# Three weight loads behind waits on VectorE, added on TensorE after each convolution chunk

## What is computed

```python
def attn(u):                                   # (8, 2048, 1024)
    x = u @ W_in + b_in                        # 1024 -> 3072
    uc = dw_causal_conv(x, short_w, short_b)   # 3 taps per channel
    q, k, v = split(uc)
    v = dw_causal_conv(k * v, inner_w, inner_b)  # 4 taps per channel
    return (q * v) @ W_out + b_out
def ffn(x):
    probs = softmax(x @ gate_w.T + gate_b)
    h = relu(x @ w1[e] + b1[e])                # for all e, 1024 -> 2048
    out = h @ w2[e] + b2[e]                    # for all e, 2048 -> 1024
    return sum over the top 2 of probs of out[e] * probs[e]
x = x + attn(layernorm(x))
x = x + ffn(layernorm(x))
```

## Time and profile before

| what | us |
|---|---|
| median of three runs | 2606.03 |
| the three runs | 2765.21, 2595.39, 2606.03 |
| the profiled execution's own time | 2595.71 |
| its span, slowest core | 2594.2 |
| spans of the eight cores | 2588.5 to 2594.2 |
| granted TensorE clock, mean of each core | 0.913 to 0.916 |
| TensorE busy with matmuls | 2214.1 (85%) |
| VectorE busy | 786.5 (30%) |
| ScalarE busy | 444.9 (17%) |

### The profile page before, as it was taken

One profiled execution on the slowest core, in us unless ns is written; L12 is line 12 of the kernel. 1 busy time (PEld: TensorE's weight loads), 2 busy tenths in 40 slices (PEclk: granted clock), 3 DMA queues, 4 the chain that ended last, 5 costly groups with the idle time before them and its releaser, 6 DMA issues.

```text
span 2594.2 us, 24806 instructions; the slowest of 8 cores (2588.5 to 2594.2 us)
## 1 busy us (share of the span) xinstructions
PE 2214.1 (85%) x9840; PEld 1020.3 (39%) x9840; DVE 786.5 (30%) x1346; ACT 444.9 (17%) x784; POOL 24.3 (1%) x81
## 2 busy tenths in 40 slices
PE   1657685622799999999999997699999999999999
PEld 1323231322344444444444444434444444444444
DVE  2086979566211111111111321211211112111121
ACT  1222121111221120211102021130201112021120
POOL 0000000000000000000000000000000000000000
PEclk9968787755799999999999996689999999999999
DMA  8300000300333334554334451033454333554331
GB/s 195 68 1 1 1 1 0 65 1 0 65 65 65 65 65 73 90 89 74 65 66 77 86 93 54 17 66 65 83 94 84 65 66 65 89 90 81 65 65 65
DMA packets 10624, 161.25 MB, mean 62 GB/s; under 512 B 1024, under 2 KB 1152, under 8 KB 6288
## 3 DMA queue, kind: packets, MB, share of 16 engines
q0 software_dynamic: 5968, 142.63, 31.0%
q1 hardware_dynamic: 4544, 17.05, 1.9%
HBM read 293.91 MB, written 8.39 MB: 117 GB/s over the span
## 4 chain that ended last, share of the span: by engine, by line
PE 79%; DVE 8%; issue 7%; DMA 3%; ACT 2%; DVEq 0%; POOL 0%; ACTq 0%; POOLq 0%
PE psum L712 17%; PE psum L757 17%; PE psum L717 17%; PE psum L759 17%; PE psum L500 4%; DMA winbt<-winl 3%; PE psum L369 2%; PE psum L615 1%; DVE tmpBt L564 1%; PE psum L618 1%; ACT ln2tft L358 1%; DVE tmpAt L544 1%; ACT ln2T L356 1%; DVE tmpBt L558 1%; DVE ln2ft L328 1%
## 5 line engine op out<-in xcount | busy, mean ns | idle before, releaser
L757 PE MATMUL psum<-w2bt,hbt 128*128 128x512 bf16 x2048 | 782.8, 382 | 0.8 <-DVE resid L766 0.8
L759 PE MATMUL psum<-w2bt,hbt 128*128 128x512 bf16 x2048 | 782.3, 382 | 0.0
L725 ACT ACTIVATE hbt<-psum,constsf_s 128x1024 bf16<-128x1024 f32 x256 | 285.3, 1114 | 1369.6 <-PE psum L717 1369.6
L712 PE MATMUL psum<-ln2T,w1bt 128*128 128x512 bf16 x2048 | 486.8, 381 | 0.7 <-ACT wbct L455 0.7
L717 PE MATMUL psum<-ln2T,w1bt 128*128 128x512 bf16 x2048 | 483.8, 379 | 0.0
L731 DVE TENSOR_TENSOR hbt<-hbt,wbct 128x1024 bf16<-128x1024 bf16 x256 | 177.3, 692 | 748.4 <-ACT hbt L725 748.4
L766 DVE TENSOR_TENSOR resid<-resid,psum 128x1024 f32<-128x1024 f32 x128 | 156.3, 1221 | 732.6 <-PE psum L759 732.6
L500 PE MATMUL psum<-ln1tt,winbt 128*128 128x512 bf16 x768 | 216.1, 449 | 145.4 <-DVE qkvt L534 104.8
L757 PEld LDWEIGHTS psum<-w2bt,hbt 128*128 128x128 bf16 x2048 | 202.7, 99 | 251.3 <-issue 15.3
L712 PEld LDWEIGHTS psum<-ln2T,w1bt 128*128 128x128 bf16 x2048 | 200.9, 98 | 245.5 <-issue 5.8
L759 PEld LDWEIGHTS psum<-w2bt,hbt 128*128 128x128 bf16 x2048 | 201.6, 98 | 242.8 <-issue 6.5
(11 more groups left out here) (68 smaller groups left out, 663.2 us busy)
## 6 DMA issues: line engine op xcount, KB each, us to landing
w1bt<-w1l POOLq DMA_DIRECT2D x16, 4096.0 KB, 27.5
w2bt<-w2l POOLq DMA_DIRECT2D x16, 4096.0 KB, 27.3
out<-resid SPq DMA_DIRECT2D x16, 512.0 KB, 2.6
winbt<-winl POOLq DMA_DIRECT2D x8, 768.0 KB, 8.4
resid<-u SPq DMA_DIRECT2D x1, 6144.0 KB, 44.3
resid<-u SPq DMA_DIRECT2D x1, 2048.0 KB, 16.9
woutbt<-woutl POOLq DMA_DIRECT2D x1, 2048.0 KB, 14.7
constsf_s<-constsf SPq DMA_DIRECT2D x1, 244.0 KB
```

What stands on the lines that cost most here:

```text
L712: T.matmul(bank(bb), lhs, ln2T[Dc][:, 0:512], start=(Dc == 0), stop=(Dc == DC - 1))
L725: em = s_s.inc(S.activation(hbuf[Hcc][:, :], bank(bb, 1024), AF.Relu, bias=constsf[:, B10 + 16 * e + Hcc:B10 + 16 * e + Hcc + 1]))
L757: T.matmul(bank(bb), lhs, w2B[Hcc][:, 0:512], start=st, stop=(Hcc == HC - 1))
L759: ins = T.matmul(bank(bb + 1), lhs, w2B[Hcc][:, 512:1024], start=st, stop=(Hcc == HC - 1))
```

## The change

A helper `warmers` is added, and `emit_conv` calls it after each chunk's y product. `ym` is the value of VectorE's counter once y is done. For the values `ym - 10`, `ym - 5` and `ym` TensorE gets a wait and then a weight load of the first 128 columns of `selB` (8 partitions, loaded at the start of the program). No matmul uses these weights: each matmul that follows brings its own load. The waits are made directly and not by `Waiter`.

```diff
+        def warmers(sem, upto, n=3, stride=5):
+            for i in range(n - 1, -1, -1):
+                v = upto - i * stride
+                if v > 0:
+                    T.wait_ge(sem.h, v)
+                    T.ldweights(selB[0:8, 0:128])
...
                 y_mark[c] = ym
                 tmp_free = ym
+                warmers(s_v, ym, 3, 5)
                 if chunk_cb is not None:
                     chunk_cb(c)
```

## The result

The changed kernel takes 2687.96 us (median of 10 runs) against 2594.83 us for the kernel before on the same chip. The ratio is 1.0354, 95% interval [1.0341, 1.0368]. The change makes the kernel 3.5% slower, 92 us by this ratio. The forecast was 2690, with a range from 2672 to 2714. Medians are over all runs, while a ratio leaves out the executions in which cores of a die ran longer at a lower granted clock, so that a ratio and the quotient of two medians can differ a little.

What follows compares the result with a forecast made beforehand. The projection's end on TensorE was taken to bound tiles 0 to 2; held behind the last y, they lose 91.9 us, giving 2687.6 from the profiled run or 2697.9 from the median; forecast 2690, range 2672 to 2714.

Steps and rivals of the forecast that it cites:

- What bounds a tile: Attention part, tiles 0 to 2: the input projection's end on TensorE sets the tile's end; delaying it delays everything.
- The waits hold the queue: Tiles 0 to 2: no next-tile projection matmul starts before the last y; 0.25 us from y's end to the first matmul.
- The rival in which a waiting load lets the matmuls pass: TensorE sets waiting weight loads aside, projection runs as before: 2596 to 2606 us, no change; chance 0.03.
- the sign that the forecast named: First projection matmul of tile 1: at 143.6 us if waits do not hold the matmuls, at 225 if they do.
- The length of a burst: After the convolution in tiles 0 to 2: 192 projection matmuls in one burst take 43.6 us.
- the slow start: First matmuls of each projection burst run slower than 0.215 us each, costing between 0 and 2.7 us; 2.0 in the sum.
- the half clock: Projection bursts at half clock throughout: 75 us for 192 matmuls, 32 more a tile, 2783 us; lower burst clock has 0.03.
- 13/16: Peak-current limit of 13/16 of the clock in the bursts: 9.5 us a tile, 2716 us; lower burst clock has 0.03.
- The loads: 96 weight loads at 0.104 us; 23 of a tile's 24 hidden, the last adds 0.1 us; 0 in tile 3.
- The clock held by the loads: Loads keep TensorE's clock at 1.00 over convolution and tile 3's gate pieces: 13 us less, 2674 us; chance 0.04.
- The sum: Delays of 30.0, 31.3 and 30.6 us in tiles 0 to 2, together 91.9, on 2595.71: 2687.6 us.

Runs made afterwards that it cites:

- the new order: Kernel before with the projection's chunks as k, v, q of each chunk in turn, instead of the eight q's last: 2562.14 us against 2596.87, ratio 0.9863.

## Why the prediction was right

- **What bounds a tile.** The step was that the end of the projection on TensorE sets the end of tiles 0 to 2. It held in both directions: ending it later by 30 us cost 92 us in three tiles, ending it about 12 us sooner gained 35 us. With the new order it stopped being so in tile 1, where VectorE's chain ends 0.81 us later.
- **The waits hold the queue.** The forecast had the 192 matmuls of a tile wait for the last y. They did, at 223.86 us on core 0, 0.38 us after y's end at 223.48. The forecast took 0.25 us, with an upper bound of 0.5. The rival in which a waiting load lets the matmuls pass has fallen by the sign that the forecast named: the first projection matmul of tile 1 starts at 223.86 us and not at 143.6. The run with waits only adds that it makes no difference whether a load or a matmul stands behind the wait.
- **The length of a burst.** 43.6 us was forecast, and 43.20, 43.80 and 43.11 were measured. Against 192 x 0.215 = 41.3 us that leaves 1.8 to 2.5 us for the slow start, inside the bound. Both cases of a lower clock in long bursts have fallen, the half clock and 13/16: the granted clock in the burst of tile 0 is 0.96, and 183 of its weight loads took 39.38 us, 0.215 each. One reading was wider than its row: the earlier trace rows is core 7 alone. In the same stretch (83.5 to 125.6 us) cores 1, 2 and 4 have 0.97. The expert part on core 7 has 0.62 from 1600 to 1700 us, around the gate of the second half. Neither changes the sum.
- **The loads.** 0.104 us each, off the path but for the last of a tile, and even that one made no more than 0.03 us of difference. Alone they cost nothing measurable. In tile 3 the forecast was 0, and 0.9993 [0.9969, 1.0018] was measured.
- **The clock held by the loads.** A rival at 0.04. The clock over the convolution fell from 0.72 to 0.50 instead of rising. The bursts beside it were gone; in the run with loads only, which has the bursts, it is 0.73.
- **The sum.** 91.9 us forecast, 92 by the ratio, 91.2 between the two spans, 93 between the two medians. By tiles it was 30.0, 31.3 and 30.6 against 29.7, 32.2 and 28.8 measured on core 0. Part of the exact fit is luck: the tiles gave 1.3 us less than forecast, and core 0 lost 2.4 us in the expert part, which the forecast had at nothing. The choice of 2690 over 2687.6 allowed for a median before of 2606.03; over ten runs it is 2594.83, and 2687.6 was the better number.

What the forecast did not see is how the loss is spread over the chunks. It spoke of the last load's wait alone. The runs with fewer chunks show that TensorE, with 192 x 0.215 = 41 us of work beside 85 us of VectorE's, can start its work four chunks late and still be in time, but not six.

## What to carry to other kernels

A wait added on an engine is priced by what is queued behind it, and not by itself. Before one adds a wait for a late event, look in the queue's order for the work that ran early there, and ask whether it fits behind the event: here 96 pairs cost 92 us ahead of the projection and at most 0.2% behind it. The same reading gives the improvement: count how many instructions of the bounding engine are left after the last event that they have to wait for, and reorder them so that few are. Then look who ends last: here VectorE's chain took over in one tile.

## What the runs showed of the hardware

- Idle matmuls with eight partitions did not lift TensorE's clock (0.50 to 0.51 over the eight cores, with TensorE busy 62% of the stretch). The same number with 128 partitions did (0.68 to 0.71). The operands' values differ too.
- In that run with 128 partitions, the 16 fp32 logit matmuls of a gate piece took 3.55 us in five of the eight pieces of core 3 although the transposes ahead of them ran in 1.07 us; on core 1 some took 1.93 to 3.24. It looks as if the high clock was often lost again while TensorE waited 2.63 us for ScalarE's copies of the transposes; that is read from these lengths and was not tested.
- Weight loads of eight partitions in a row, without waits, took 0.05 us each (24 in 1.23 and 1.22 us), half of the 0.10 that a single one shows.
